# A three-block transformer layer over 32 tiles: tiles counted from the other end, half of one expert pass moved in among the last tiles, and a value product in half-precision parts

## The reference

```
h  = LN(softmax(x Wq (x Wk)^T, causal) x Wv + x)          # self attention
c  = LN(softmax(h Wcq (ctx Wck)^T) ctx Wcv + h)           # attention over the context
x1 = x + relu(LN(relu(c W1 + b1) + c))
x2 = x1 + (16 causal heads of width 32, decayed weights) Wproj
s  = LN(silu(n sw1) * (n sw2)) sw3, n = LN(x2)            # shared feed-forward
out = x2 + s, except for rows x[index_b, index_t]:
      x2 + s * shared_w + expert_w * out_of_expert[argmax(sigmoid(n eg_w) + bias)]
```

## Time and profile before

| what | value |
| --- | --- |
| time, median of 3 runs | 1496.43 us (1494.0 to 1496.84) |
| profiled execution: its time | 1495.49 us |
| profiled execution: its span | 1493.6 us |
| mean granted TensorE clock | 0.987 |
| TensorE busy, weight loads busy | 94%, 59% |
| DVE, ACT, POOL busy | 74%, 36%, 32% |

### The profile page before, as it was taken

How to read it: one execution, slowest core, us unless ns; L and a number is a source line. 1 busy time by engine, 2 the same in 40 slices (tenths; PEclk the granted TensorE clock), 3 DMA queues, 4 the chain that set the end, 5 groups by cost and what they waited for, 6 DMA issues and landing times.

```text
span 1493.6 us, 32437 instructions
## 1 busy us (share of the span) xinstructions
PE 1401.0 (94%) x13668; PEld 883.8 (59%) x13668; DVE 1101.4 (74%) x2215; ACT 530.6 (36%) x979; POOL 480.4 (32%) x499
## 2 busy tenths in 40 slices
PE   7779999999999999999999999999999999999789
PEld 3346666666565666666666566666656666665444
DVE  6667777777777777787777777777777777777645
ACT  2533333334333333333333333333433333343221
POOL 0033333333333333333333333333333333333211
PEclk9899999999999999999999999999999999999899
DMA  9632344333233344433323234444323324434530
GB/s 349 251 119 79 135 142 142 142 141 125 96 129 110 110 142 142 142 142 137 107 109 131 97 131 142 142 142 142 130 97 123 117 104 142 142 135 163 190 108 22
DMA packets 38657, 201.37 MB, mean 135 GB/s; under 512 B 5096, under 2 KB 5992, under 8 KB 28400
## 3 DMA queue, kind: packets, MB, share of 16 engines
q1 hardware_dynamic: 37792, 199.19, 37.2%
q10 hardware_dynamic: 720, 0.10, 0.0%
HBM read 182.24 MB, written 17.04 MB: 133 GB/s over the span
## 4 chain that ended last, share of the span: by engine, by line
PE 60%; DVE 22%; issue 9%; POOL 4%; ACT 3%; DMA 1%; SPq 0%; DVEq 0%; POOLq 0%; ACTq 0%
PE ps_a L1476 8%; PE ps_a L1442 8%; PE ps_t L1476 7%; PE ps_t L1434 6%; DVE stats L1005 4%; PE ps_a L1453 4%; PE ps_a L1517 4%; PE ps_a L1488 4%; POOL rstd L575 4%; PE ps_t L1453 4%; PE ps_v L1453 3%; DVE kbd L1126 3%; PE ps_a L1462 2%; PE ps_t L1488 2%; PE ps_a L1498 2%
## 5 line engine op out<-in xcount | busy, mean ns | idle before, releaser
L575 POOL TENSOR_TENSOR rstd<-var,mhalf 128x1 f32<-128x1 f32 x224 | 183.9, 821 | 444.2 <-DVE var L1007 444.0
L584 POOL TENSOR_TENSOR act_l<-act_t,act_h 128x512 f16<-128x512 f32 (+1 forms) x154 | 171.1, 1111 | 349.6 <-ACT act_t L696 261.1
L688 ACT ACTIVATE act_h<-ps_t,scale 128x512 f16<-128x512 f32 (+1 forms) x110 | 71.1, 646 | 176.7 <-PE ps_t L1434 176.7
L584 POOL TENSOR_TENSOR last_slot<-last_slot 128x512 f16<-128x512 f32 (+1 forms) x70 | 77.4, 1106 | 153.6 <-ACT last_slot L696 114.1
L1126 DVE TENSOR_SCALAR kbd<-ps_a,unscale 32x512 f32<-32x512 f32 x64 | 48.2, 754 | 54.9 <-PE ps_a L1488 53.8
L1442 PE MATMUL ps_a<-wcv,act_t 128*128 128x512 f32 x176 | 82.1, 610 | 2.2 <-ACT act_t L702 2.2
L1005 DVE BATCH_NORM_STATS2 stats<-rows 128x6 f32<-128x512 f32 x110 | 76.4, 695 | 3.8
L1434 PE MATMUL ps_t<-ident,rows 128*128 128x128 f32 x352 | 57.4, 286 | 19.7 <-DVE rows L1011 19.5
L696 ACT ACTIVATE act_t<-ps_t,scale 128x512 f32<-128x512 f32 (+1 forms) x110 | 70.3, 639 | 0.2 <-PE ps_t L1434 0.2
L1453 PE MATMUL ps_a<-w_parts,act_h 128*128 128x512 f16 x264 | 65.0, 383 | 1.3 <-ACT act_h L688 1.3
L1166 DVE STREAM_TRANSPOSE pbd<-rows 32x512 f32<-32x512 f32 x88 | 61.8, 703 | 2.8
(11 more groups left out here) (369 smaller groups left out, 3291.8 us busy)
## 6 DMA issues: line engine op xcount, KB each, us to landing
ctx_t<-in_ctx_t SPq DMA_DIRECT2D x32, 2056.0 KB, 8.1
ctx_n<-in_ctx_n SPq DMA_DIRECT2D x32, 2048.0 KB
ctx_last<-in_ctx_last SPq DMA_DIRECT2D x32, 256.0 KB
x_in<-in_x SPq DMA_DIRECT2D x22, 256.0 KB, 7.2
x_scratch<-rows SPq DMA_DIRECT2D x22, 256.0 KB, 8.7
out<-rows SPq DMA_DIRECT2D x22, 256.0 KB, 2.0
wattn<-in_ew SPq DMA_DIRECT2D x6, 512.0 KB, 5.6
out<-last_slot SPq DMA_DIRECT2D x11, 256.0 KB, 2.0
```

What stands on the lines that cost most here:

```text
L575: nc.gpsimd.tensor_tensor(rstd[s][:], var[s][:], mhalf[:], ALU.pow).then_inc(rstd_ready[s], 1)
L584: nc.gpsimd.tensor_tensor(act_l[s][:, chunks], act_t[s][:, chunks], act_h[s][:, chunks], ALU.subtract).then_inc(act_l_ready[s], 1)
L688: nc.scalar.activation(act_h[s][:, 0:width // P].rearrange("p c r -> p (c r)"), bank[s][:, 0:width], ACT.Copy, scale=scale[:, k:k + 1]).th ...
```

## The change

1. **Tiles in opposite order.** Tile n of the pipeline loads and stores array row `FINAL - n`, so the tile with chosen rows is worked first, and its x2 and out are in memory long before the end. The list of tiles to redo leaves it out; each entry of the list is now half a pass (experts 0 to 3 or 4 to 7).
2. **The first half of its pass among the last two tiles' units.** New units `e_moments`, `e_norm`, `e_turn`, `e_logits`, `e_gate_a/b/c`, `e_in0..3`, `e_bias`, `e_z`, `e_zn`, `e_zt`, `e_out`, `e_total` stand in `LAST`, for rounds 32 and 33. The sum goes through the slot that tile 29 has left (`ps_a`, `ps_t` of that slot). The loop behind the pipeline does the second half: 4 experts for this tile.
3. **No fill-in matmuls** (`keep_clock` is gone).
4. **The loop's form.** Weights of both halves lie in one `arena` and are addressed by a register (`half_of`). Sigmoid and SiLU become Tanh with scale 0.5. The next tile's turn, gate and choice stand at the end of the loop; next rows' `expert_in(0)` is not made ahead any more. ACT issues the load of the next x2. The first expert's step has three more DVE operations of 128x512 on `o` and `old`, for halves.
5. **Context values in half parts.** `wcv` gets parts of its own (`K_WCV`, `LOW_WCV`: a maximum in the third group, a high part by ACT, `set_wcv`, a low part by DVE, `set_14b`; its load moves ahead of `wproj` and `w3`). Per tile: ACT sums the magnitudes of each row (`context_sum`), DVE makes a scale of that sum (`context_scaled`, three small steps), ACT multiplies the rows by it, `turn_w` turns them, ACT writes them twice, POOL makes the remainder, TensorE does `high` and `low`.
6. **Orders.** `FIRST`, `ORDER` and `LAST` are written anew around this. `turn_pc` moves from the end of a round behind the next `ffn_out_l`, `project_v_l` ahead of `turn_w`, POOL's `silu` and `turn_z` to the end of the round.

The core of the diff:

```diff
 ORDER = {
-    "pe": [(3, "ffn_out"), (3, "ffn_out_l"), (2, "project_q_l"), (1, "context_mix"), (2, "head_scores"),
-        (0, "turn_xn"), (2, "project_v"), (0, "project_self"), (1, "turn_w"), (0, "project_self_l"),
-        (1, "context_out"), (2, "project_v_l"), (0, "self_scores"), (0, "value_self"), (0, "value_self_l"),
-        (0, "turn_p"), (2, "head_mix"), (1, "turn_h2"), (0, "self_mix"), (2, "project_out"), (2, "project_out_l"),
+    "pe": [(3, "ffn_out"), (3, "ffn_out_l"), (1, "turn_pc"), (2, "project_q_l"), (1, "context_mix"),
+        (2, "head_scores"), (0, "turn_xn"), (2, "project_v"), (0, "project_self"), (0, "project_self_l"),
+        (2, "project_v_l"), (1, "turn_w"), (0, "self_scores"), (1, "context_out"), (1, "context_out_l"),
+        (0, "value_self"), (0, "value_self_l"), (0, "turn_p"), (2, "head_mix"), (0, "self_mix"), (2, "project_out"),
+        (1, "turn_h2"), (2, "project_out_l"), (1, "hidden"), (1, "hidden_l"), (0, "turn_h"), (2, "turn_x2n"),
...
 LAST = {
+    "pe": [(2, "project_k_l"), (3, "ffn_out"), (3, "ffn_out_l"), (1, "turn_pc"), (2, "project_q_l"), (2, "e_zt1"),
+        (1, "context_mix"), (2, "head_scores"), (2, "e_in3"), (0, "turn_xn"), (2, "project_v"), (2, "project_v_l"),
+        (1, "turn_w"), (2, "e_out1"), (0, "project_self"), (1, "e_turn"), (0, "project_self_l"), (1, "e_logits"),
+        (0, "value_self"), (1, "e_in0"), (0, "self_scores"), (2, "e_zt2"), (1, "context_out"), (1, "context_out_l"),
+        (0, "value_self_l"), (0, "turn_p"), (2, "head_mix"), (1, "e_in1"), (0, "self_mix"), (2, "e_out2"),
+        (2, "project_out"), (2, "project_out_l"), (1, "e_zt0"), (2, "e_zt3"), (2, "e_out3"), (1, "turn_h2"),
+        (1, "hidden"), (0, "turn_h"), (1, "hidden_l"), (1, "e_in2"), (0, "project_query"), (2, "turn_x2n"),
+        (1, "e_out0"), (0, "project_query_l"), (0, "context_scores"), (2, "ffn_in"), (2, "ffn_in_l"),
+        (1, "turn_x1n"), (1, "project_k"), (1, "project_q"), (2, "turn_z")],
...
-                    sp.dma_start(x_in[s][:], a["x"][tile]).then_inc(x_loaded[s], 16)
+                    sp.dma_start(x_in[s][:], a["x"][FINAL - tile]).then_inc(x_loaded[s], 16)
...
+                def context_sum(s, r, tile):
+                    act.wait_ge(v_ready[s], 4 * r + 2)
+                    nc.scalar.activation(flat_rows(act_h[s]).bitcast(BF16), v_n[s][:], ACT.Abs, accum_out=row_sum[s][:]
+                                         ).then_inc(row_summed[s], 1)
+
+                def context_scaled(s, r, tile):
+                    act.wait_ge(inv_ready[s], 3 * r + 2)
+                    nc.scalar.activation(v_n[s][:], v_n[s][:], ACT.Copy, scale=row_scale[s][:]).then_inc(v_ready[s], 1)
...
+                def context_scaled(s, r, tile):
+                    chain = Chain("context_scaled", s, r)
+                    dve.wait_ge(row_summed[s], r + 1)
+                    chain(nc.vector.tensor_scalar(row_sum[s][:], row_sum[s][:], 1e-30, 0.5 ** SCALED_TOP, ALU.max,
+                                                  ALU.mult))
+                    nc.vector.reciprocal(row_scale[s][:], row_sum[s][:]).then_inc(inv_ready[s], 1)
...
-                    product32(ps_a[s][:], act_t[s], wcv).then_inc(rows_done[s], 1)
...
+                    "context_out": after(LOW_WCV, high(ps_a, 3, wcv)), "context_out_l": low(ps_a, 3, wcv, rows_done),
...
-                def keep_clock(s, r, tile):
...
+                def e_in(k):
+                    def unit(s, r, tile):
+                        if tile == FINAL:
+                            pe.wait_ge(xn_t_ready, 1)
+                            pe.wait_ge(part_loaded[k // 3], PART_COUNTS[k // 3])
+                            if k:
+                                pe.wait_ge(e_u_ready, k)
+                            else:
+                                pe.wait_ge(out_ready[s_a], r_a + 1)
...
-                for q in range(4):
-                    pe.wait_ge(part_loaded[q], PART_COUNTS[q])
-                count = tiles_to_do(pe)
+                pe.wait_ge(part_loaded[3], PART_COUNTS[3])
+                pe.wait_ge(bias_loaded, 16 * (1 + EH))
+                count = passes_to_do(pe)
                 with pe.Fori(0, count) as i:
+                    half = half_of(pe, i)
...
+                    expert_in(0)
                     expert_in(1)
...
-                    for k in range(NE):
-                        pe.wait_ge(e_z_ready, NE * i + k + 1)
+                    for k in range(EH):
+                        if k == EH - 1:
+                            turn_expert_rows(ps_t[s_last], i + 2)
+                        pe.wait_ge(e_z_ready, EH * (i + 1) + k + 1)
...
-                        if k == NEXT_ROWS + 1:
-                            gate_logits(i + 2)
-                    expert_in(0)
```

More of the change, by code:

```diff
@@ L73 @@
 FIRST = {
[L74 to L90, removed]
@@ L147 @@
+    "pool": [(2, "turn_x1n"), (3, "silu"), (3, "turn_z"), (0, "xn_moments"), (0, "turn_xn"), (1, "e_norm"),
+        (2, "e_zn2"), (1, "turn_w"), (2, "head_scores"), (1, "e_zn0"), (2, "head_mix"), (2, "e_zn3"),
+        (1, "context_out"), (0, "self_mix"), (2, "project_out"), (1, "turn_h2"), (0, "turn_h"), (1, "e_zn1"),
+        (1, "hidden"), (2, "turn_x2n"), (1, "out_norm")],
 }
 LOADS = [(0, "load_x"), (0, "set_first"), (0, "set_rest"), (0, "load_ctx_t"),
-         (3, "store_x2"), (3, "first_x2"),
@@ L1231, in first_rows, with e_norm @@
-                        assert steps[0] == E_FIRST
+                        expert_moments(before, x2[:])
+                def e_norm(s, r, tile):
+                    if tile == FINAL:
+                        dve.wait_ge(turned[s_a], 7 * (r_a + 1))
                         dve.wait_ge(e_rstd_ready, 1)
@@ L1614, in _ @@
                     "context_scores": context_scores, "turn_pc": turn_pc, "context_mix": context_mix,
-                    "turn_w": turn(ps_t, v_n, v_ready, 3, 2), "context_out": context_out,
-                    "turn_h2": turn(ps_t, rows1, rows_ready, 6, 3), "hidden": after(LOW_W1, high(ps_a, 3, w1)),
-                    "hidden_l": low(ps_a, 3, w1, rows_done), "turn_x1n": turn(ps_t, rows1, rows_ready, 6, 4),
-                    "project_k": after(LOW_K, high_t(ps_a, 4, wattn, D)), "project_k_l": low_t(ps_a, 4, wattn, k_done, D),
@@ L1624, in _ @@
-                    "ffn_in_l": low(ps_a, 6, w12, rows_done), "turn_z": turn(ps_t, v_n, rows_ready, 6, 6, HC, H),
-                    "ffn_out": after(LOW_W3, high(ps_a, 7, w3, chunks=HC)), "ffn_out_l": low(ps_a, 7, w3, rows_done, chunks=HC),
+                    "turn_w": turn(ps_t, v_n, v_ready, 4, 3),
+                    "context_out": after(LOW_WCV, high(ps_a, 3, wcv)), "context_out_l": low(ps_a, 3, wcv, rows_done),
+                    "turn_h2": turn(ps_t, rows1, rows_ready, 6, 3), "hidden": after(LOW_W1, high(ps_a, 4, w1)),
@@ new lines, in _ @@
+                    "hidden_l": low(ps_a, 4, w1, rows_done), "turn_x1n": turn(ps_t, rows1, rows_ready, 6, 4),
+                    "project_k": after(LOW_K, high_t(ps_a, 5, wattn, D)), "project_k_l": low_t(ps_a, 5, wattn, k_done, D),
+                    "project_q": after(LOW_Q, high_t(ps_t, 5, wattn, 0, whole=5)), "project_q_l": low_t(ps_t, 5, wattn, q_done, 0),
+                    "project_v": after(LOW_V, project_v), "project_v_l": low(value_bank, 5, wattn, v_done, 2 * D),
+                    "head_scores": head_scores, "head_mix": head_mix, "project_out": after(LOW_WPROJ, high(ps_a, 6, wproj)),
@@ L1626, in _ @@
+                    "project_out_l": low(ps_a, 6, wproj, rows_done),
+                    "turn_x2n": turn(ps_t, rows1, rows_ready, 6, 5), "ffn_in": after(LOW_W12, high(ps_a, 7, w12)),
+                    "ffn_in_l": low(ps_a, 7, w12, rows_done), "turn_z": turn(ps_t, v_n, rows_ready, 6, 6, HC, H),
+                    "ffn_out": after(LOW_W3, high(ps_a, 8, w3, chunks=HC)), "ffn_out_l": low(ps_a, 8, w3, rows_done, chunks=HC),
                     "set_01": peaks_turn(0), "set_02": set_02, "set_03": peaks_out(0), "set_04": set_04, "set_05": set_05,
```

764 lines of the change are left out of this document (465 added, 299 removed), and 4 rows, old and new, of the table FIRST.

## The result

| | before | after |
| --- | --- | --- |
| time, median | 1495.78 us (4 runs, 1494.0 to 1496.84) | 1476.24 us (4 runs, 1475.63 to 1476.32) |
| ratio | | 0.987, 95% interval 0.9853 to 0.9887 |
| span of the profiled execution | 1493.6 us | 1474.5 us |
| DVE, ACT, POOL busy | 74%, 36%, 32% | 77%, 40%, 36% |

A forecast was written before the change was run, and what follows sets the result against it. TensorE's work bounds steady rounds and the expert pass, chains of waits the last rounds. Terms -26, +2, +4.5 and -20.5 sum to -40: 1455.5 from 1495.5, forecast 1456 us as median, range 1443 to 1474.

The forecast's parts named there:

- The value product and the round: Steady rounds: the value product in half parts takes 0.87 us less a tile, -26 us (-15 to -36).
- Rival 2: Steady rounds: row scales give the gain back, remainder or scaling late by about 0.9 us; 1482 us, chance 0.10.
- Rival 4: Steady rounds: the new order also removes waits, another -15 to -20 us; 1438 us, chance 0.10.
- Rival 5: Steady rounds: slower, ACT's scaling passes queue so `turn_w` is late every round; 2.5 us new waits, 1505 us, chance 0.04.
- All but the first and last rounds, 30 tiles, work at this pace.: Pipeline: step that applies the 0.87 us gain a tile to 30 tiles, giving -26 us.
- The last rounds, +4.5: Last tiles' rounds: four experts added, fill-ins removed, DVE delays and low clock; +4.5 us (-4 to +13).
- Rival 1: Last rounds don't take the work in, DVE's queue delays the last tile; +13 to +16 us, 1465 to 1468, chance 0.16.
- The loop, -20.5: From the end of `ffn_out_l` to the end: 34.4 us against 54.7, -20.5 us (-24 to -15).
- 3.4 for `expert_in(0)`, 4.8 for its chain and 2.1 for three of 0.7 on `o` put inside it: z0 at 11.3.: Loop's head: after 1 us for entry, these lengths in series put z of expert 0 at 11.3 us.
- Rival 3: Low clock through the loop, 22 us of TensorE work at half rate; +18 to +20 us, 1475, chance 0.05.
- The start, +2: First rounds: new high and low weight parts, less a shorter first value product; +2 us (-1.4 to +6).
- The signs of being wrong: Prediction is wrong if the steady round isn't 40.6 to 41.0 us, or the last rounds grow by over 8.

The follow-up runs named there:

- experiment 4: The changed kernel with the context's value product in full precision again, orders, row scales and expert pass kept: 1507.44 us, ratio 1.0101.
- experiment 1: The changed kernel with the table `LAST` in force from round 32, so rounds 30 and 31 run in the steady order: 1473.39 us, ratio 0.9857.
- experiment 5: Experiment 1 with the load of row x2 for the first half pass issued ahead of the expert weights' loads: 1468.82 us, ratio 0.9821.
- experiment 2: The changed kernel with ACT making the tanh of expert 0 ahead of the turned coefficients' copy in the loop: 1473.97 us, ratio 0.9865.
- experiment 6: Experiment 5 with experiment 2's edit, and ACT's issue of the next row's load moved behind the tanh of expert 1: 1465.15 us, ratio 0.9797.
- experiment 9: Experiment 8 with the three DVE operations on the output row moved behind the bias of expert 1: 1458.41 us, ratio 0.976.
- experiment 3: The changed kernel with fill-in matmuls (`keep_clock`) put back ahead of the loop: 1477.2 us, ratio 0.9881.
- experiment 7: The changed kernel with rounds 2 and 3 in the steady order, their set-up units at their places: 1468.79 us, ratio 0.9826.
- experiment 8: The changed kernel with all edits that gained together, those of experiments 1, 5, 6 and 7: 1458.53 us, ratio 0.9757.

## Why the prediction was half right

- **The value product and the round.** Right, and for its reason: 0.84 less a round (0.87 forecast), no wait ahead of `turn_w` or of the low part, and experiment 4 gives the half parts 1.00. Rivals 2, 4 and 5 fall.
- **"All but the first and last rounds, 30 tiles, work at this pace."** This step failed. 26 of 28 rounds do. Two run in the table `LAST` without the units that it was made for, and take 43.3 us: +3.3 against before instead of -1.7 (experiment 1). I had read `LAST_FROM` in the code and taken the last table as an order for expert units, without laying out one round of it without them. The rest of this term's miss is in the cut and in the average round, as above.
- **The last rounds, +4.5, measured +7.6.** The term's mechanism was right and it was mis-sized. I laid out DVE's queue and not SP's, where the row's load stands behind the experts' weights, nor POOL's remainder, beside which DVE's step ahead of `e_turn` took 1.39 us for 0.55. With both gone the term is +5.7 (experiment 5). Rival 1 (+13 to +16) falls.
- **The loop, -20.5, measured -13.6.** This is the second step that failed: "3.4 for `expert_in(0)`, 4.8 for its chain and 2.1 for three of 0.7 on `o` put inside it: z0 at 11.3." z 0 came 16.0 us after the last product. I costed the chain by DVE's rows and left out ACT's queue, in which the tanh stands behind a copy that waits for TensorE's second product: TensorE's wait is 2.8 us longer for it and the loop 2.3 (experiment 2). The load's issue cost 1.2 us more, and with it 0.8 of low clock at the end went (38.2 in experiment 2, 36.2 in experiment 6). The three operations were sized rightly, 2.1 in the sum: in the changed kernel the stretch from L1366 to L1370, where they stand, takes 2.87 us for z 0 and 0.92 for z 1, so 1.95 is theirs. They can't be had for nothing by moving them: 1.15 us of wait comes back ahead of z 1 (experiment 9).
- **Low clock** is the rest of the loop's miss: 9.46 for two products that take 7.13 at best, 4.84 for one of 3.60. Rival 3 had the mechanism and five times the price (18 to 20 us). In the one trace with fill-ins, what they returned in one place was lost in the next two (experiment 3).
- **The start, +2, measured +4.7.** Its sign was luck. I had costed the new parts of the weights and the later first value product. That product does come late (84.49 against 79.74, forecast near 82), but at the turn of x1 of tile 0 0.5 us of it is left (106.85 against 106.34), and at `context_mix` of round 2 nothing (113.16 against 114.95; 0.9 of this lead is `project_q_l`, which now stands behind it). With the steady order in rounds 2 and 3 the mark of round 4 is at 199.49 against 200.26 before, though that execution was ahead by 0.9 at 25 us already, behind the first loads. So the +4.7 is the new table in rounds 2 and 3, which I left out: 45.2 us from mark to mark against 41.9 in the first of them (experiment 7).
- **Rival 5's price.** Its sum is wrong: 2.5 us of new waits in 30 rounds on a forecast of 1456 are 1531, and 1505 takes the 0.87 off a second time. No such wait came, so nothing hangs on it.
- **The signs of being wrong.** Neither of the two came true: the round is 40.84 and the last rounds grew by 7.6. They looked at neither rounds 30 and 31 nor the loop, where 5.0 and 6.9 us of the miss lie.

With the orders repaired the same change takes 1458.5 us. The sum of durations forecast 1456: what it lacked was mostly the queues' order in rounds that it didn't lay out, and for the rest low clock.

## What to carry to other kernels

When work is moved into an order written by hand, lay out by the rows each round in which that order is in force, those without the new units too, and every queue of it, a small copy on ACT and a load on SP included. Where a row names an engine as the releaser, go one step further back: a wait of 4.2 us "for DVE" was for its greater part a transfer that stood behind six larger ones. Compare two kernels by a mark only where the same work stands ahead of it in both. Leave fill-in work against a low clock for last, and judge it by the whole time.

## What was not expected of the hardware

The same waits don't give the same clock. Ahead of the loop all variants but experiment 3 have a wait of 4.1 us, then one of 0.57 and one of 0.6 to 0.7, with the same work between. The two products in behind them (16 recorded matmuls) took 9.46, 9.86, 9.49, 9.38, 9.43, 9.42 and 8.99 us in seven kernels, and 7.13 in experiments 7 and 8, each in one execution. Executions of one kernel differ too: 3 us and 0.981 to 0.987 of mean clock in experiment 7. Behind a wait of 1.53 us one product in took 3.60 in experiments 2 and 6, and 5.08 in experiment 8. The Trainium skill, TensorE: Matmul & The Clock Gate, "What's actually happening", has activity release the throttle; the slow stretches in these rows all lie behind waits. From the length of a wait alone, these rows don't allow a forecast of whether the stretch behind it will be slow. What came before goes along with it: where the first two products took 7.13 (experiments 3, 7 and 8), the product behind the next wait took 6.04, 5.34 and 5.08; where they took 8.99 or more, it took 4.80 to 5.04 behind a wait of 4.36 or 4.37, and 3.60 behind 1.53 or none. So experiments 7 and 8 show, without any fill-ins, the same shift of cost to the next place as experiment 3. Why it is so isn't shown.
